# Moving the mask sign, two wide scalings and the centring of weight rows from VectorE to ScalarE, with a new order of the first two tiles

## The chip, the cores and the metric

The kernel runs on one core of one Trainium2 chip. It is one launch. The metric is the device time of one execution in microseconds (us). The engines are named as in the profile: PE is TensorE, ACT is ScalarE, DVE is VectorE, POOL is GpSimd and SP is SyncE, which issues all DMAs of this kernel.

## The reference

Three residual layers over x (128 sequences of 32 rows of 1024), all in float32:

```
x = x + cross_attention(layernorm(x), ctx, ctx, mask)   # 32 query heads, 8 key/value heads, 257 keys
x = x + s4(layernorm(x))                                # causal convolution along the 1024 features + D*u
x = x + router_ffn(layernorm(x), A_w, B_w, Wq_w, keys)  # 64 experts of rank 8, top 16, softmax gates
```

- Attention: scores = q k^T / sqrt(32) + mask, softmax over 257 keys, times the values. The context (128, 257, 256) is key and value at once.
- S4: a kernel of 1024 taps is computed from Lambda, p, q, V, B, Ct and the step: a Cauchy sum over 64 states at 1024 roots of unity, then an inverse FFT. It is then convolved causally with each row.
- FFN: z = x A_w^T (512 columns), gated by expert, times B_w^T, times 2. The router is x Wq_w^T keys^T. The kernel takes the mean of each row of A_w and Wq_w away beforehand, so that the layernorm's mean needs no pass of its own.

## The kernel before

**Tiles.** Four sequences make a tile of 128 rows, and there are 32 tiles. For each tile the attention runs in four parts, b = 0 to 3, one for each sequence. `scores(it, b)` is 24 matmuls into the four banks of `ps_s` (three products of a high and a low part of q and k). Then DVE does eight steps `maximum(it, n)` (line 1395: add the mask, store, and take the row's extreme), ACT does eight `exp(it, n)` (line 832), PE turns the result (`pair_chunk`, line 565), ACT copies it out of PSUM (`pair_copy`, line 784) and PE multiplies by the values (`attend`, line 597). `scores(it, b+1)` waits until all eight maxima of part b have been taken, since they read the same banks.

**Stages.** In the steady part (`for it in range(HEAD, TAIL)`, tiles 2 to 30) the attention of tile it runs beside the convolution of tile it-1 and the FFN of tile it-2. The order inside is written out by hand, engine by engine; there is no scheduler at run time. What stands ahead of that loop on each engine is a list of calls, also written out, for tiles 0 and 1 and for the set-up work: the S4 kernel (`s4_step()` takes the next piece of the DVE generator `s4_kernel`), the router product, and the 16 turned half blocks of A_w and B_w (`weight_chunk(j, h)`, then `weight_high` on ACT and `weight_low` on DVE). Each engine works through its own list in order and waits on semaphores, so an instruction whose input is late holds everything behind it on that engine.

**What the change touches.**

- `masks` (line 1200, DVE): changes the sign of the mask.
- `query_means` and `weight_mean(j)` (lines 793 and 806, ACT): a copy in place whose accumulator gives each row's mean. `query_centre` and `weight_centre(j)` (lines 1218 and 1223, DVE) then scale the row back by 1024 and subtract the mean.
- In `s4_kernel` (DVE) the two scalings `w0 = br*lr` and `w1 = br*li` (line 1271, `times`), 128 by 512 each. Behind them stand the two scaled additions (line 1268), the squares and their sum (line 1250), a reciprocal of 128 by 512 (line 1309) and two products, after which `cauchy_sums` (line 523, PE) can run.
- `STAGE` names the three buffers in which weight rows land: `x`, `xr` and `ots` in the profile. `BANKS` says into which of the four PSUM banks `ps_p` each product goes.
- The query path of tile 0: x lands in `xq`, `q_stats` (DVE), `row_scale` (POOL), `q_norm` (ACT), `store_q` and `move_q` (SP, through DRAM), `q_turn` (DVE), `q_high` (ACT), `q_low` (POOL). In between, POOL takes the product with the 257th key (`last_product`, `last_sum`, `last_mask`), whose result goes through DRAM (`store_last`, `turn_last`) to the first maximum.

Of the kernel before, what the change touches and what calls it, by code (L numbers as in the profile page):

```python
# [18 lines left out]
ALU = mybir.AluOpType  # L19
# [33 lines left out]
S4 = {"cauchy": 31, "sums": 33, "hat": 71, "dft": 72, "column": 77, "rows": 78}  # L53
# [23 lines left out]
    "keys": (1,),  # L77
    "router": (2,),
    "sums": (2,),
    "dft": (1,),  # L80
    "rows": (0,),
    "strip": (1, 3, 0,),
    "w": (1, 0, 1, 3, 2, 1, 0, 2, 3, 2, 2, 3, 0, 2, 2, 2,),
# [27 lines left out]
def build(nc, io):  # L111
    ctx = ExitStack()
    with ctx:
# [136 lines left out]
        su_step = sem("su_step")  # L250
        su_s4 = sem("su_s4")
# [63 lines left out]
        def _(sp):  # L315
# [176 lines left out]
        def _(pe):  # L492
# [252 lines left out]
            keys_transpose(); router_product(); weight_chunk(0, 0); weight_chunk(0, 1); weight_chunk(1, 0)  # L745
            scores(0, 0); weight_chunk(1, 1); scores(0, 1); cauchy_sums(); pair_chunk(0, 0); pair_chunk(0, 1)
# [444 lines left out]
        def _(dve):  # L1191
# [530 lines left out]
```

## Time and profile before

| | us |
|---|---|
| median of 3 runs | 1307.82 |
| lowest and highest | 1303.91, 1310.32 |
| the profiled execution | 1306.38 |
| its span in the profile | 1304.6 |
| PE busy in the span | 1243.8 (95%) |
| ACT busy | 1117.4 (86%) |
| DVE busy | 1057.6 (81%) |
| POOL busy | 827.7 (63%) |

The span is the stretch between the first and the last instruction; the execution's time is 1.8 us longer. The share of busy time is an average over the start, the steady part and the end. In the profile's 40 slices of 32.6 us each, PE stands at 2, 5 and 7 tenths in the first three and at 9 from the fourth on. TensorE's granted clock is at full speed in all slices but the second (9 tenths) and the third (7 tenths).

### The profile page before, as it was taken

The numbers are of one execution on the slowest core, as the hardware profiler recorded it, in microseconds if no ns is written. First come the engines' busy times: TensorE is split into PE (matmuls) and PEld (weight loads), VectorE is DVE, ScalarE is ACT, GpSimd is POOL, SyncE is SP. The second block draws the span as 40 slices with busy tenths as digits, with TensorE's granted clock in tenths as the row PEclk, the third lists the DMA queues.
The fourth block names the chain that finished last, engine by engine and source line by source line (L and its number), as shares of the span: only waits on it lengthen the run. The fifth ranks groups of instructions, "written<-read, shape, count | busy, mean of one in ns | idle before, by whom it ended". The sixth has DMA issues, their size and how long they took to land.

```text
span 1304.6 us, 42153 instructions
## 1 busy us (share of the span) xinstructions
PE 1243.8 (95%) x13676; PEld 1078.2 (83%) x13676; DVE 1057.6 (81%) x3560; ACT 1117.4 (86%) x3329; POOL 827.7 (63%) x1259
## 2 busy tenths in 40 slices
PE   2579999999999999999999999999999999999997
PEld 2457888888888888888888888888888888888876
DVE  6988888888888887888888888887888888888753
ACT  3689989989999998999999898988999898998841
POOL 5437667666666776666677666667766666776420
PEclk9979999999999999999999999999999999999999
DMA  8544454454455455445545454454545445554210
GB/s 211 138 121 121 136 150 121 128 145 130 124 133 140 121 136 137 134 125 131 137 120 146 127 148 117 125 137 128 141 125 145 125 121 141 127 142 120 61 59 33
DMA packets 270940, 166.45 MB, mean 128 GB/s; under 512 B 195433, under 2 KB 253298, under 8 KB 270722
## 3 DMA queue, kind: packets, MB, share of 16 engines
q1 hardware_dynamic: 270722, 163.74, 46.7%
q8 instruction: 112, 1.84, 0.6%
q14 instruction: 106, 0.87, 0.2%
HBM read 128.50 MB, written 34.08 MB: 125 GB/s over the span
## 4 chain that ended last, share of the span: by engine, by line
PE 85%; DVE 4%; SPq 3%; ACT 2%; issue 2%; DMA 2%; POOL 1%; DVEq 0%; POOLq 0%; ACTq 0%
PE ps_p L565 25%; PE ps_p L651 15%; PE ps_p L636 15%; PE ps_p L664 14%; PE ps_p L597 9%; PE ps_s L577 8%; SPq L384 2%; ACT pr L832 1%; DVE ms L1395 1%; DMA dn<-den 1%; DMA turn<-lasts 1%; DVE x L1250 0%; POOL lastp L1095 0%; ACT pts L784 0%; SPq L431 0%
## 5 line engine op out<-in xcount | busy, mean ns | idle before, releaser
L832 ACT ACTIVATE pr<-ms,negmax 128x256 f32<-128x256 f32 x1024 | 513.9, 504 | 12.0 <-DVE negmax L1395 11.9
L1395 DVE CUSTOM_DVE_ANT_0 ms<-ps_s,neg_mask,last 128x256 f32<-128x256 f32 x1024 | 456.6, 470 | 35.4 <-PE ps_s L577 29.9
L784 ACT ACTIVATE pts<-ps_p 128x512 f32<-128x512 f32 x512 | 295.9, 592 | 48.3 <-PE ps_p L565 44.2
L565 PE MATMUL ps_p<-ident,pr 128*128 128x128 f32 x2048 | 306.2, 278 | 9.4 <-DVE wa_lo L1195 4.5
L565 PEld LDWEIGHTS ps_p<-ident,pr 128*128 128x128 f32 x2048 | 240.1, 141 | 44.7 <-issue 16.7
L832 ACT ACTIVATION_READ_ACCUMULATOR pr<-ms,negmax 128x1 f32 x1024 | 199.8, 195 | 0.0
L1053 POOL TENSOR_TENSOR kt<-kr,kt 128x512 fp32r<-128x512 f32 x128 | 165.1, 1290 | 28.4 <-ACT kt L784 27.9
L651 PE MATMUL ps_p<-wa_hi,ut_hi 128*128 128x288 f32 x512 | 177.6, 347 | 1.6 <-DVE ut_lo L1195 1.6
L651 PE MATMUL ps_p<-wa_lo,ut_hi 128*128 128x288 f32 x512 | 151.2, 295 | 0.0
L651 PE MATMUL ps_p<-wa_hi,ut_lo 128*128 128x288 f32 x512 | 150.6, 294 | 0.0
L1095 POOL TENSOR_TENSOR lastp<-lastp 128x256 f32<-128x256 f32 (+4 forms) x320 | 129.7, 405 | 22.7
L597 PE MATMUL ps_p<-pts,cx 128*32 128x128 f32 x4096 | 139.2, 277 | 0.1
L636 PE MATMUL ps_p<-strip_hi,ut_hi 128*128 128x512 f32 (+2 forms) x384 | 138.3, 360 | 0.4 <-DVE tmp L1485 0.4
L577 PE MATMUL ps_s<-kt,qs 32*128 32x256 f32 x3072 | 127.8, 297 | 8.0 <-DVE negmax L1395 5.7
L636 PE MATMUL ps_p<-strip_hi,ut_lo 128*128 128x512 f32 (+2 forms) x384 | 133.4, 347 | 0.0
L636 PE MATMUL ps_p<-strip_lo,ut_hi 128*128 128x512 f32 (+2 forms) x384 | 133.3, 347 | 0.0
L1076 POOL TENSOR_TENSOR qs<-qr,qs 128x512 fp32r<-128x512 f32 x64 | 83.3, 1301 | 69.9 <-ACT qs L784 69.9
L577 PEld LDWEIGHTS ps_s<-kt,qs 32*128 32x128 f32 x3072 | 101.5, 187 | 30.0 <-issue 29.8
L784 ACT ACTIVATE ut_hi<-ps_p 128x512 fp32r<-128x512 f32 x128 | 76.2, 595 | 56.5 <-PE ps_p L565 56.4
L597 PEld LDWEIGHTS ps_p<-pts,cx 128*32 128x32 f32 x4096 | 104.6, 110 | 21.4 <-issue 16.1
L1060 POOL TENSOR_SCALAR lns<-lns 128x1 f32<-128x1 f32 x96 | 18.4, 192 | 158.2 <-DVE lns L1434 157.9
L664 PE MATMUL ps_p<-wb_hi,zt_hi 128*128 128x512 f32 x256 | 111.7, 436 | 3.0 <-DVE zt_lo L1195 3.0
(140 smaller groups left out, 2717.3 us busy)
## 6 DMA issues: line engine op xcount, KB each, us to landing
kx<-in_ctx SPq DMA_DIRECT2D x512, 64.0 KB, 2.4
cx<-in_ctx SPq DMA_DIRECT2D x128, 256.0 KB, 3.1
xq<-in_x SPq DMA_DIRECT2D x32, 512.0 KB, 4.3
turn_q<-xq SPq DMA_DIRECT2D x32, 512.0 KB, 3.8
qx<-turn_q SPq DMA_DIRECT2D x128, 128.0 KB, 2.9
xr<-in_x SPq DMA_DIRECT2D x32, 512.0 KB, 4.3
out_x<-tmp SPq DMA_DIRECT2D x32, 512.0 KB, 5.2
dn<-den SPq DMA_DIRECT2D x512, 2.0 KB, 2.2
```

What stands on the lines that cost most here:

```text
L565: mm = pe.transpose(into[:, j * P:(j + 1) * P], source, ident[:, :])
L577: mm = pe.matmul(ps_s[:, quad, h * SW:(h + 1) * SW], qs[rs, it % 2, q_part, b, h, :, :].rearrange("p r s -> p (r s)"), kt[rs, b, k_part, h ...
L597: mm = pe.matmul(product("o", b, it)[HEAD_DIM * q:HEAD_DIM * (q + 1), h * P:(h + 1) * P], cx[:, b, j, g * HEAD_DIM:(g + 1) * HEAD_DIM], pt ...
L636: mm = pe.matmul(product("y", k, tile)[:, o0:512], u[:, c, :], s[:, s0:s0 + w], start=(c == 0 and j == 0), stop=(c == 4 * k + 3 and j == 2 ...
L651: mm = pe.matmul(product("f", k, tile)[:, 0:ZB], u[:, c, :], w[:, c, k * ZB:(k + 1) * ZB], start=(c == 0 and j == 0), stop=(c == FC - 1 an ...
L664: mm = pe.matmul(product("b", k, tile)[:, :], u[:, c, :], w[:, c, k * 512:(k + 1) * 512], start=(c == 0 and j == 0), stop=(c == BC - 1 and ...
L784: return act.activation(out, in_, ACT.Copy, scale=scale)
L832: act.activation(pr[:, b % 2, g, :], ms[:, n % MS, :], ACT.Exp, bias=negmax[:, n % MS:n % MS + 1], scale=-1.0, accum_out=den[:, b, g:g + 1 ...
L1053: pool.tensor_tensor(kt[:, b, 1, :, 0:2 * P], kr[:, :, :], kt[:, b, 0, :, 0:2 * P].bitcast(F32), ALU.subtract).then_inc(kl_done, 1)
L1076: pool.tensor_tensor(qs[:, tile % 2, 1, :, h, :, :], qr[:, :, :, :], qs[:, tile % 2, 0, :, h, :, :].bitcast(F32), ALU.subtract).then_inc(q ...
L1095: pool.tensor_tensor(near, near, far, ALU.add).then_inc(ls_done, 1)
L1395: dve.tensor_tensor_reduce(ms[:, n % MS, :], ps_s[:, g % GPH, g // GPH * SW:(g // GPH + 1) * SW], neg_mask[:, 0:SW], 1.0, last[:, it % 2, ...
```

## The change

- The mask's sign, the centring of Wq_w and of the four blocks of A_w, and the two wide scalings leave DVE for ACT. The mean is now accumulated with a negative sign, and the centring is `Identity(-1024 * row + bias)`. The scalings are a `Copy` with a scale from `lam`, signalled by a new semaphore `su_wide`, on which DVE waits ahead of the two scaled additions.
- The written lists of all five engines for tiles 0 and 1 are replaced, with the banks of the set-up products and the tile-0 strips. The steady loop and the end are the same as before.

```diff
-S4 = {"cauchy": 31, "sums": 33, "hat": 71, "dft": 72, "column": 77, "rows": 78}
+S4 = {"cauchy": 29, "sums": 31, "hat": 69, "dft": 70, "column": 75, "rows": 76}
...
-    "w": (1, 0, 1, 3, 2, 1, 0, 2, 3, 2, 2, 3, 0, 2, 2, 2,),
+    "w": (0, 2, 0, 1, 2, 3, 2, 2, 3, 2, 1, 2, 3, 0, 1, 3,),
...
-            load_x(0); load_s4(); load_weight(0); load_router(); load_keys(0, 0); load_mask(); clear_kernel()
-            load_wide(); load_last(0); load_weight(1); store_q(0); load_keys(0, 1); load_weight(2); move_q(0)
-            load_keys(0, 2); store_last(0); load_weight(3); load_context(0, 0); load_keys(0, 3); load_x(1)
...
+            load_s4(); load_x(0); load_router(); load_wide(); load_context(0, 2); load_mask(); load_keys(0, 0)
+            load_last(0); load_weight(0); load_keys(0, 1); store_q(0); clear_kernel(); load_weight(1)
+            load_weight(2); move_q(0); load_x(1); load_keys(0, 2); load_weight(3); store_last(0); load_context(0, 0)
+            turn_last(0); load_keys(0, 3); load_context(0, 3); load_last(1); load_keys(1, 0); store_q(1)
+            load_weight(4); load_keys(1, 1); move_q(1); load_x(2); load_context(0, 1); move_den(0, 0)
+            load_weight(5); load_keys(1, 2); load_weight(6); load_weight(7); store_last(1); load_keys(1, 3)
...
             def query_means():
                 act.wait_ge(router_loaded, 32)
-                act.activation(wq_sb, wq_sb, ACT.Copy, scale=1.0 / DIM,
+                act.activation(wq_sb, wq_sb, ACT.Copy, scale=-1.0 / DIM,
                                accum_out=row_mean[0:ROUTER, BC:BC + 1]).then_inc(query_mean, 1)
+
+            def masks():
+                act.wait_ge(m_loaded, 16)
+                copy(neg_mask[:, :], mask_raw, -1.0).then_inc(su_mask, 1)
+
+            def query_centre():
+                act.wait_ge(query_mean, 1)
+                act.activation(wq_sb, wq_sb, ACT.Identity, scale=-float(DIM),
+                               bias=row_mean[0:ROUTER, BC:BC + 1]).then_inc(query_centred, 1)
+
+            def weight_centre(j):
+                act.wait_ge(a_mean, j + 1)
+                act.activation(stages[STAGE[j]], stages[STAGE[j]], ACT.Identity, scale=-float(DIM),
+                               bias=row_mean[:, j:j + 1]).then_inc(a_centred, 1)
+
+            def wide_products():
+                act.wait_ge(wide_loaded, 32)
+                act.wait_ge(su_s4, 2)
+                for j in range(2):
+                    act.activation(work[j], wide[2], ACT.Copy, scale=lam[:, j:j + 1]).then_inc(su_wide, 1)
...
-            def masks():
-                dve.wait_ge(m_loaded, 16)
-                dve.tensor_scalar(neg_mask[:, :], mask_raw, -1.0, None, ALU.mult).then_inc(su_mask, 1)
-                dve.wait_ge(su_mask, 1)
...
-            def query_centre():
-                dve.wait_ge(query_mean, 1)
-                dve.tensor_scalar(wq_sb, wq_sb, float(DIM), row_mean[0:ROUTER, BC:BC + 1], ALU.mult,
-                                  ALU.subtract).then_inc(query_centred, 1)
-
-            def weight_centre(j):
-                dve.wait_ge(a_mean, j + 1)
-                dve.tensor_scalar(stages[STAGE[j]], stages[STAGE[j]], float(DIM), row_mean[:, j:j + 1], ALU.mult,
-                                  ALU.subtract).then_inc(a_centred, 1)
...
-                dve.wait_ge(wide_loaded, 32)
                 ar, ai, br, bi = wide
                 w0, w1 = work
                 lr, li = lam[:, 0:1], lam[:, 1:2]
-                times(w0, br, lr)
-                times(w1, br, li)
-                yield
+                dve.wait_ge(su_wide, 2)
                 scaled(w0, bi, li, w0, ALU.subtract)
                 scaled(w1, bi, lr, w1, ALU.add)
                 yield
```

PE's list up to the second group of scores, before. The names are the outputs and inputs of each instruction; line 513 is the router product, 565 with `x`, `xr`, `ots` a turned weight block, 577 the scores, 523 the Cauchy sums:

```order
L513 MATMUL ps_p<-zg,pts 128x64 x8
L565 MATMUL ps_p<-ident,x 128x128 x8
L565 MATMUL ps_p<-ident,xr 128x128 x4
L577 MATMUL ps_s<-kt,qs 128x256 x24
L565 MATMUL ps_p<-ident,xr 128x128 x4
L577 MATMUL ps_s<-kt,qs 128x256 x24
L523 MATMUL ps_p<-x 128x16 x8
```

The same place now, where line numbers are one higher:

```order
L514 MATMUL ps_p<-zg,pts 128x64 x8
L566 MATMUL ps_p<-ident,x 128x128 x8
L524 MATMUL ps_p<-x 128x16 x8
L566 MATMUL ps_p<-ident,xr 128x128 x8
L578 MATMUL ps_s<-kt,qs 128x256 x24
L566 MATMUL ps_p<-ident,ots 128x128 x4
L566 MATMUL ps_p<-ident,pr 128x128 x4
L566 MATMUL ps_p<-ident,ots 128x128 x4
L566 MATMUL ps_p<-ident,pr 128x128 x4
L578 MATMUL ps_s<-kt,qs 128x256 x24
```

The Cauchy sums and both halves of weight block 1 now stand ahead of the first scores, and block 2 (`ots`) ahead of the second.

ACT's list around the first exponential (line 832 before, 853 now); 806 and 827 are means, 808 a centring, 846 and 867 the normalisation of the queries, 784 and 785 copies. Before:

```order
L806 ACTIVATE ots,top<-ots 128x1024
L784 ACTIVATE kt<-kr 128x512
L784 ACTIVATE qs<-qr 128x4x128
L832 ACTIVATE pr,den<-ms,negmax 128x256
L784 ACTIVATE wa_hi<-ps_p 128x4x128 x2
L784 ACTIVATE kt<-kr 128x512
```

Now:

```order
L808 ACTIVATE xr<-xr,top 128x1024
L785 ACTIVATE qs<-qr 128x4x128
L785 ACTIVATE wa_hi<-ps_p 128x4x128
L827 ACTIVATE ots,top<-ots 128x1024
L785 ACTIVATE qs<-qr 128x4x128
L827 ACTIVATE x,top<-x 128x1024
L808 ACTIVATE ots<-ots,top 128x1024
L785 ACTIVATE wa_hi<-ps_p 128x4x128
L867 ACTIVATE xq<-xq,lns 128x512
L785 ACTIVATE wa_hi<-ps_p 128x4x128
L785 ACTIVATE kt<-kr 128x512
L853 ACTIVATE pr,den<-ms,negmax 128x256 x2
```

The fourth mean (`x`), three of the four centrings, block 1's two copies and half of tile 1's normalisation stand ahead of the first exponential now. At the very start of ACT's list, `wide_products` stands ahead of tile 0's normalisation.

DVE's list up to the first maximum (line 1395 before, 1401 now), from the first turn of the queries, before:

```order
L1408 STREAM_TRANSPOSE qr<-qx 128x512
L1223 TENSOR_SCALAR xr<-xr,top 128x1024
L1250 TENSOR_TENSOR un<-un 128x512
L1309 RECIPROCAL un<-un 128x512
L1431 BN_STATS lns<-xq 128x6 x2
L1395 ISA ms,negmax<-ps_s,neg_mask,last 128x256
```

Now:

```order
L1313 RECIPROCAL un<-un 128x512
L1408 STREAM_TRANSPOSE kr<-kx 128x8x2x32
L1414 STREAM_TRANSPOSE qr<-qx 128x512
L1217 TENSOR_TENSOR wa_lo<-ps_p,wa_hi 128x8x64
L1257 TENSOR_TENSOR x<-x,un 128x512 x2
L1437 BN_STATS lns<-xq 128x6
L1217 TENSOR_TENSOR wa_lo<-ps_p,wa_hi 128x4x128 x2
L1414 STREAM_TRANSPOSE qr<-qx 128x512
L1322 COPY x<-ps_p 128x8x4 x2
```

The whole chain of the S4 kernel up to the Cauchy sums now stands ahead of the second turn of the queries (the second `qr` row), where before it stood behind it.

## Rows read from the trace of the kernel before

**Rows 1.** Windows: span stretch, busy PE, PEld, DVE, ACT, POOL, PEclk, DMA share, GB/s.
```profile
0.00:37.00 37.00, 9.72 (x57) 7.95 (x57) 26.58 (x47) 11.88 (x21) 19.39 (x34) 1.00 0.82 203
37.00:80.00 43.00, 26.87 (x245) 22.97 (x249) 41.37 (x136) 35.35 (x103) 17.63 (x29) 0.83 0.47 126
80.00:116.00 36.00, 31.69 (x365) 24.08 (x354) 28.16 (x93) 32.31 (x97) 23.25 (x36) 0.91 0.53 142
180.00:220.00 40.00, 40.00 (x442) 34.69 (x444) 33.52 (x112) 36.35 (x110) 27.85 (x43) 1.00 0.45 125
```

**Rows 2.** Timeline of PE: start, us, instruction, idle before and its releaser.
```profile
30.79 1.11 PE L565 MATMUL ps_p<-ident,xr 128*128 128x128 f32 x4 [11.02 <-DVE xr L1223]
31.96 1.66 PE L577 MATMUL ps_s<-kt,qs 32*128 32x256 f32 x24
...
42.20 3.60 PE L523 MATMUL ps_p<-x 128*128 128x16 f32 x16 [0.17 <-DVE x L1250]
...
77.79 1.65 PE L577 MATMUL ps_s<-kt,qs 32*128 32x256 f32 x24 [2.21 <-POOL qs L1076]
...
116.23 0.98 PE L577 MATMUL ps_s<-kt,qs 32*128 32x256 f32 x24
```

**Rows 3.** The removed DVE instructions by line: duration ns min/median/max, first and last start.
```profile
L1218 DVE TENSOR_SCALAR pts<-pts,top x1: 741/741/741, 10.7 to 10.7; 16x1024 f32<-16x1024 f32 x1
L1200 DVE TENSOR_SCALAR neg_mask<-ms x1: 298/298/298, 13.2 to 13.2; 128x257 f32<-128x257 f32 x1
L1271 DVE TENSOR_SCALAR un<-tmp,x x2: 1262/1315/1368, 13.9 to 15.2; 128x512 f32<-128x512 f32 x2
L1223 DVE TENSOR_SCALAR x<-x,top x2: 1215/1412/1609, 16.5 to 48.4; 128x1024 f32<-128x1024 f32 x2
L1223 DVE TENSOR_SCALAR xr<-xr,top x1: 1410/1410/1410, 29.3 to 29.3; 128x1024 f32<-128x1024 f32 x1
L1223 DVE TENSOR_SCALAR ots<-ots,top x1: 1798/1798/1798, 42.5 to 42.5; 128x1024 f32<-128x1024 f32 x1
```

**Rows 4.** ACT's means and normalisations by line, same columns.
```profile
L806 ACT ACTIVATE x<-x x2: 1040/1042/1044, 10.5 to 43.9; 128x1024 f32<-128x1024 f32 x2
L846 ACT ACTIVATE xq<-xq,lns x4: 797/800/803, 11.6 to 47.3; 128x512 f32<-128x512 f32 x4
```

**Rows 5.** Timeline of DVE, 13 to 53 us.
```profile
17.68 1.72 DVE L1268 SCALAR_TENSOR_TENSOR un<-tmp,x,un 128x512 f32<-128x512 f32 x2
19.31 0.70 DVE L1402 STREAM_TRANSPOSE kr<-kx 128x512 f32<-128x512 f32 x1
...
24.22 1.40 DVE L1250 TENSOR_TENSOR un<-x 128x512 f32<-128x512 f32 x2
...
30.66 1.75 DVE L1250 TENSOR_TENSOR un<-un 128x512 f32<-128x512 f32 x1
32.44 3.35 DVE L1309 RECIPROCAL un<-un 128x512 f32<-128x512 f32 x1
...
36.85 0.47 DVE L1395 CUSTOM_DVE_ANT_0 ms<-ps_s,neg_mask,last 128x256 f32<-128x256 f32 x1
...
40.78 1.37 DVE L1250 TENSOR_TENSOR x<-x,un 128x512 f32<-128x512 f32 x2
...
50.75 1.46 DVE L1250 TENSOR_TENSOR x<-x 128x8 f32<-128x8 f32 x6
```

**Rows 6.** Issues of DMAs in the first 14 us: KB each, median us to landing.
```profile
tmp<-in_wide SPq DMA_DIRECT2D x1, 512.0 KB, 6.8
```

**Rows 7.** Timeline of ACT at the first exponential.
```profile
37.36 0.51 ACT L832 ACTIVATE pr<-ms,negmax 128x256 f32<-128x256 f32 x1 [7.29 <-DVE negmax L1395]
...
37.87 0.58 ACT L784 ACTIVATE wa_hi<-ps_p 128x512 fp32r<-128x512 f32 x1
```

**Rows 8.** ACT's waits from 36 to 125 us: total, times, longest.
```profile
ACT pr L832 <- DVE negmax L1395: 9.6, 6, 7.3
ACT kt L784 <- DVE kr L1402: 2.2, 2, 2.0
```

More of the change, by code:

```diff
@@ L76 @@
     "o": (3, 2, 1, 1,),
[L77 to L82, printed above, removed]
-    "w": (1, 0, 1, 3, 2, 1, 0, 2, 3, 2, 2, 3, 0, 2, 2, 2,),
+    "keys": (3,),
+    "router": (3,),
+    "sums": (1,),
+    "dft": (0,),
+    "rows": (1,),
+    "strip": (2, 3, 2,),
+    "w": (0, 2, 0, 1, 2, 3, 2, 2, 3, 2, 1, 2, 3, 0, 1, 3,),
 }
@@ L250, in build @@
         su_step = sem("su_step")
+        su_wide = sem("su_wide")
         su_s4 = sem("su_s4")
@@ new lines, in _ @@
+            weight_chunk(1, 0); weight_chunk(1, 1); scores(0, 0); weight_chunk(2, 0); pair_chunk(0, 0)
+            weight_chunk(2, 1); pair_chunk(0, 1); scores(0, 1); weight_chunk(3, 0); pair_chunk(0, 2)
+            pair_chunk(0, 3); weight_chunk(3, 1); pair_chunk(0, 4); weight_chunk(4, 0); scores(0, 2)
+            weight_chunk(4, 1); attend(0, 0); attend(0, 1); pair_chunk(0, 5); pair_chunk(0, 6); weight_chunk(5, 0)
+            weight_chunk(5, 1); pair_chunk(0, 7); dft_product(); pair_chunk(0, 8); scores(0, 3); weight_chunk(6, 0)
@@ L760, in _ @@
+            pair_chunk(1, 4); attend(1, 0); attend(1, 1); pair_chunk(1, 5); pair_chunk(1, 6); pair_chunk(1, 7)
+            pair_chunk(1, 8); attend(1, 2); attend(1, 3); u_chunk(0, 0); scores(1, 3); u_chunk(0, 1)
+            pair_chunk(1, 9); convolve(0, 0, 0, 4); convolve(0, 1, 0, 2); pair_chunk(1, 10); convolve(0, 1, 2, 8)
+            z_chunk(0, 0, 0); z_chunk(0, 1, 0)
             for it in range(HEAD, TAIL):
@@ L1017, in _ @@
-            exp(1, 20); exp(1, 21); q_high(2, 0); exp(1, 22); last_exp(1, 1); exp(1, 23); pair_copy(1, 9)
-            exp(1, 24); k_high(2, 1); exp(1, 25); pair_copy(1, 10); exp(1, 26); q_high(2, 1); exp(1, 27); exp(1, 28)
-            exp(1, 29); z_high(0, 0); exp(1, 30); z_high(0, 1); last_exp(1, 2); exp(1, 31); pair_copy(1, 11)
-            last_exp(1, 3); k_high(2, 2)
+            step_exp(); query_means(); keys_copy(); wide_products(); q_norm(0, 0); q_norm(0, 1); masks()
+            query_centre(); k_high(0, 0); weight_mean(0); weight_centre(0); router_high(); weight_high(0, 0)
@@ new lines, in _ @@
+            weight_mean(1); k_high(0, 1); weight_centre(1); q_high(0, 0); weight_high(0, 1); weight_mean(2)
+            q_high(0, 1); weight_mean(3); weight_centre(2); weight_high(1, 0); q_norm(1, 0); weight_high(1, 1)
+            k_high(0, 2); exp(0, 0); exp(0, 1); weight_high(2, 0); q_norm(1, 1); exp(0, 2); exp(0, 3)
+            weight_centre(3); k_high(0, 3); pair_copy(0, 0); exp(0, 4); exp(0, 5); pair_copy(0, 1)
+            weight_high(2, 1); exp(0, 6); pair_copy(0, 2); exp(0, 7); weight_high(3, 0); exp(0, 8); last_exp(0, 0)
@@ L1021, in _ @@
+            exp(1, 22); k_high(2, 1); exp(1, 23); exp(1, 24); exp(1, 25); exp(1, 26); exp(1, 27); last_exp(1, 2)
+            q_high(2, 1); pair_copy(1, 10); exp(1, 28); exp(1, 29); z_high(0, 0); exp(1, 30); z_high(0, 1)
+            exp(1, 31); k_high(2, 2); pair_copy(1, 11); last_exp(1, 3)
             for it in range(HEAD, TAIL):
@@ L1392, in maximum @@
                     dve.wait_ge(e_done, at(it, STEPS, n + 1 - MS))
+                if it == 0 and n == 0:
+                    dve.wait_ge(su_mask, 1)
                 if it == 0 and n == 2:
@@ new lines, in _ @@
+            q_stats(2, 0); maximum(1, 0); weight_low(6, 1); maximum(1, 1); maximum(1, 2); maximum(1, 3)
+            maximum(1, 4); weight_low(7, 0); k_turn(1, 2); maximum(1, 5); maximum(1, 6); maximum(1, 7)
+            q_stats(2, 1); q_stats(2, 2); k_turn(1, 3); strip_low(0); maximum(1, 8); normalisers(0); maximum(1, 9)
+            maximum(1, 10); k_turn(2, 0); maximum(1, 11); maximum(1, 12); maximum(1, 13); maximum(1, 14)
+            strip_low(1); maximum(1, 15); strip_low(2); out_half(0, 0); maximum(1, 16); out_half(0, 1)
@@ L1653, in _ @@
+            z_low(0, 1)
             for it in range(HEAD, TAIL):
```

122 lines of the change are left out of this document (49 added, 73 removed).

## The prediction

> **What bounds the kernel now.** I read the windows first. In the steady part PE is busy for all of 40.00 us out of 40, while DVE has 33.52 and ACT 36.35: PE is the bound there [rows 1]. The change leaves that loop alone, so all it can do is bring the start of the loop forward or put it back. The loop begins where PE starts the scores of tile 2, at 116.23 us [rows 2]. Until 116 us PE is busy for 9.72 + 26.87 + 31.69 = 68.3 us only, so some 48 us of the start is waiting [rows 1]. That is the stock from which anything can be gained.
>
> The windows also say who fills the start. From 0 to 37 us nobody is full: this is latency, of DMAs and of chains from engine to engine. From 37 to 80 us DVE is busy 41.37 of 43 us, and it is the bound. From 80 to 116 us ACT takes over with 32.31 of 36, PE is at 31.69 and DVE at 28.16 [rows 1]. ACT's own waits after 36 us agree: 9.6 us for DVE's maxima, 7.3 of them ahead of the very first exponential, and 2.2 us for turned keys, again from DVE [rows 7, 8]. So a us taken from DVE before 80 us should move everything behind it, as long as ACT can follow.
>
> **What leaves DVE.** The centring of Wq_w 0.74, the mask 0.30, two scalings of 1.315, and the centrings of A_w 1.22 + 1.41 + 1.80 + 1.61: 9.71 us in eight instructions [rows 3]. Of these 1.80 and 1.61 stand behind the first maximum, at 42.5 and 48.4 us, in the stretch where DVE is the bound: 3.4 us. The other 6.3 us stand before it.
>
> **What ACT gets.** A mean over 1024 columns is 1.04 us without pointer operands, the normalisation of 512 columns with two of them 0.80 [rows 4]. A centring has one, so it lies between 1.04 and about 1.3 (1.04 plus the 0.3 by which 0.80 exceeds half of a mean, 0.52); I take 1.1, five times 5.5 us. The scalings have one pointer and 512 columns: between 0.52 and 0.80, I take 0.6 each, 1.2 us. The mask is at most the 0.51 us of an exponential of about that width [rows 7]. Together about 7 us. Up to 37 us ACT is busy 11.88 us only [rows 1], and all but one centring stand there, so they are covered; the fourth (1.1 us) stands behind the first exponentials. If that cover were gone, the 7 us would be paid whole.
>
> **The new start.** Two chains meet at the first scores.
> 1. S4 chain. The second wide table took 6.8 us from issue to landing [rows 6]. It is issued as the seventh transfer now, at about 3.6 us, and the first A_w block, the keys and the mask no longer stand ahead of it: landing near 10, with 9 and 13.9 (today's first scaling) as bounds. ACT's scalings end near 11.2. DVE then needs 1.72 (two scaled additions), 0.70 (a turn), about 1.5 for two more additions (taken as less than the 1.72), 1.40 (squares), 1.75 (their sum), 3.35 (reciprocal), two turns of 0.70, a low part as wide as a turn, 0.7, and 1.37 (two products) [rows 5]: 13.9 us, so 25 us. The first of those turns of queries may still wait for the queries to come back from DRAM; I add 1.5 for it, between 0 and 3, so 26.5. PE's Cauchy sums take 3.60, two half blocks 1.11 each and the scores 1.66 [rows 2]: 34.0.
> 2. Query chain. It ends today at 31.96 with the scores [rows 2]. POOL's key part moves behind its product with the last key, ACT's normalisation behind the scalings, and DVE's second turn behind the two products; I take the same 31 to 32, so it is not the later one.
>
> The first maximum comes at 34.4 instead of 36.85 [rows 5]: 2.4 us. Today it waits for DVE itself, which is in the reciprocal (32.44 to 35.7) while the scores have long been there [rows 2, 5].
>
> **What is ahead by then.** At 34.4 us DVE has done more than before at 36.85: the two products 1.37, the first complex product 1.46 [rows 5], one low part 0.7 and two small copies of the sums, between 0 and 0.5, taken as 0.4: together 3.9 us. With the 3.4 us that never come, DVE's lead is 2.4 + 3.9 + 3.4 = 9.7 us through the stretch that it bounds.
>
> ACT must follow. Its first exponential comes at about 35.1 instead of 37.36 [rows 7], 2.3 us. Ahead of it stand a mean 1.04, half a normalisation 0.80 and two copies of 0.58 that stood behind it [rows 4, 7], and behind it one centring of 1.1 more: 3.0 - 1.1, another 1.9 us, taken as 1.8 since ACT's instructions overlap a little. That makes 4.1. The other 5.6 us must come from ACT's waits: between 37 and 80 us it is idle for 43 - 35.35 = 7.65 us [rows 1], and most of that is for work of DVE, which comes earlier now. So 9.7 is possible without ACT being full, and from 80 us ACT has 3.7 us more of idle time [rows 1] as a reserve. PE has 16 us idle from 37 to 80, and its 3.60 us of Cauchy sums have left that stretch. I take 9.5 us, since new waits for PSUM banks (half blocks and pairs share four, and each block's bank is freed by a low part on DVE) eat a little. The upper end is 9.7 plus the reserve, 13; the lower end, if ACT recovers half of the 5.6, is 6.9.
>
> **A rule against it.** The two scalings took 1.26 and 1.37 us, while the mask, half as wide, took 0.30 [rows 3]: by width alone they would be about 0.6 each. They ran beside POOL. The Trainium skill (SBUF — State Buffer, "SBUF: two separate sides") says that VectorE and GpSimd share one pair of ports, and that the first to come holds it for its whole instruction, against single-input VectorE instructions in a fast mode as against those with two SBUF inputs, while ScalarE has ports of its own. By that rule ScalarE's 0.6 is safe, but the scaled additions behind, with two inputs in SBUF, inherit the wait.
>
> **The sum.** The profiled execution took 1306.38 us; less 9.5 that is 1296.9. The median of the runs is 1.4 us above it, so by the median 1298.3, which I predict; the rivals' times are by the median too.
>
> **The rivals.**
> - *Inherited port waits.* Of the 9.7 us that leave DVE, 2.63 - 1.2 = 1.4 for the scalings, and 1.80 + 1.61 + 1.41 - 3 x 1.22 = 1.2 for the centrings, were not the instructions' own work [rows 3]. If the next instruction waits in their place, 2.6 us come back: a gain of 6.9, 1300.9. For it: 1.72 for two scaled additions against 1.40 for two squares [rows 5]. Against it: POOL is busy 17.63 of 43 us in the stretch that counts [rows 1]. Chance 0.15.
> - *PE or SP as the new head of the line.* PE turns weight blocks ahead of scores now, and blocks 5 to 7 are issued by SP behind `load_x(2)`, which waits for POOL's product of tile 1. If block 5 is late, PE stands in front of it with pairs, the DFT and the fourth scores behind. The price is one landing, 5 to 6 us, bounded by the 6.8 of such a transfer [rows 6]: a gain of 3.5 to 4.5, 1304. For it: today 11.02 us of PE's waiting are for one weight block [rows 2]. Chance 0.18.
> - *The lead is given back at the loop's door.* If ACT (32.31 of 36 [rows 1]) cannot shorten its stretch, because its waits there are for PE's strips, the maxima run ahead and stop after eight. Gain 0 to 3: 1306.3 in the middle. Chance 0.10.
> - *Slower.* ACT's head. `wide_products` stands ahead of tile 0's normalisation, and the fourth mean and tile 1's normalisation ahead of the first exponential. If the wide table lands as late as today (13.9 [rows 3]) the normalisation moves by 3.5 us, then the turns of the queries; if the fourth block lands 5 us after the scores, exp(0,0) starts at about 44. From there ACT's own 67.7 us of work up to 116 us [rows 1], less 1.8, end at 110 plus the waits; with today's 11.3 us of waits kept, the loop starts at 121, 5 us late: 1313. It decides from exp(0,0) at 39.2 on if no wait goes, and from 50 on if all go. Against it: 37 us in which ACT is one third busy. Chance 0.07.
>
> **How the numbers follow.** The forecast has 0.50: 1298.3, on its own from 1294.8 (13 us) to 1300.9 (6.9 us). The rest is with the four rivals. A measurement tells about 0.5% from nothing, that is 6.5 us, so faster means under 1301.3. The forecast gives 0.46 to faster and 0.04 to the same; the port waits give 0.09 and 0.06, the late block 0.03 and 0.15, the returned lead 0 and 0.10, and the slower rival 0.02 to the same and 0.05 to slower. Faster 0.58, same 0.37, slower 0.05. The range reaches down to 1294.5, the 13 us end, and up to 1305.5, where the slower rival and most of the returned lead are left out.
>
> **What would show it.** Right: the scores of tile 2 start near 107 us; the first maximum near 34.4 and the first exponential near 35; Cauchy sums on PE near 26.5; DVE below nine tenths nowhere between 37 and 70; the scores of tile 1, today at 77.79 [rows 2], near 68. Wrong: a first maximum later than 37, a wait of PE for a weight block's DMA over 3 us, scaled additions over 2.5 us the pair, or a lead at tile 1's scores that is gone at tile 2's. If the lead is there at tile 2 and the time does not show it, the steady part has changed, which I exclude, since its lists are the same.

## The result

The kernel after the change took 1293.14 us in the median of 4 runs (1291.56 to 1294.01); the kernel before, run beside it, 1306.57 us (4 runs). The ratio is 0.9894, with a 95% interval of 0.9866 to 0.9922: faster by about 1.1%. The prediction was 1298.3 us with a range from 1294.5 to 1305.5. The direction is right; the gain is larger than forecast, and the time lies 1.4 us below the range. The same kernel timed a second time gave 1291.18 us against 1302.46, ratio 0.9912 [0.9896, 0.9929]. By the two comparisons the gain is 13.4 and 11.3 us. The forecast was 9.5. Single executions of one kernel lie up to 9 us apart, so 1 to 2 us between two of them say little by themselves.

### The profile after

The profiled execution took 1292.63 us, its span is 1290.8 us. The windows (stretch of the span, length, then busy time of PE, PEld, DVE, ACT and POOL with counts, PEclk, DMA share, GB/s) answer to [rows 1]:

```profile
0.00:37.00 37.00, 15.85 (x85) 13.72 (x85) 28.42 (x67) 23.61 (x43) 20.33 (x39) 1.00 0.80 220
37.00:80.00 43.00, 30.14 (x366) 23.15 (x367) 37.56 (x138) 39.95 (x124) 19.30 (x32) 0.92 0.60 148
80.00:116.00 36.00, 30.63 (x372) 25.95 (x374) 29.98 (x101) 33.74 (x101) 26.83 (x41) 1.00 0.48 129
180.00:220.00 40.00, 40.00 (x472) 34.68 (x465) 33.96 (x113) 36.11 (x111) 27.12 (x41) 1.00 0.51 127
```

In the first 37 us PE and ACT do 6.1 and 11.7 us more work than in [rows 1]. From 37 to 80 us DVE has come down from 41.37 to 37.56 us, and ACT has risen from 35.35 to 39.95 of 43. The steady part is as full of PE as before. PE's timeline (start, us, instruction, in brackets the idle time before it and its releaser) answers to [rows 2]:

```profile
25.23 3.60 PE L524 MATMUL ps_p<-x 128*128 128x16 f32 x16 [5.73 <-DVE x L1257]
28.66 1.95 PE L566 MATMUL ps_p<-ident,xr 128*128 128x128 f32 x8
30.54 1.65 PE L578 MATMUL ps_s<-kt,qs 32*128 32x256 f32 x24
...
66.27 0.99 PE L578 MATMUL ps_s<-kt,qs 32*128 32x256 f32 x24
...
104.61 0.98 PE L578 MATMUL ps_s<-kt,qs 32*128 32x256 f32 x24
```

The Cauchy sums moved from 42.20 to 25.23 us, ahead of the first scores. The scores of tile 1 start 11.5 us earlier than in [rows 2], those of tile 2, where the loop begins, 11.6 us earlier. DVE's timeline, which answers to [rows 5]:

```profile
11.06 1.54 DVE L1275 SCALAR_TENSOR_TENSOR un<-tmp,x,un 128x512 f32<-128x512 f32 x2 [1.63 <-ACT un L815]
12.63 0.71 DVE L1408 STREAM_TRANSPOSE kr<-kx 128x512 f32<-128x512 f32 x1
13.27 2.38 DVE L1275 SCALAR_TENSOR_TENSOR x<-x,un 128x512 f32<-128x512 f32 x2
15.69 1.97 DVE L1257 TENSOR_TENSOR un<-x 128x512 f32<-128x512 f32 x2
17.69 0.70 DVE L1257 TENSOR_TENSOR un<-un 128x512 f32<-128x512 f32 x1
18.42 3.35 DVE L1313 RECIPROCAL un<-un 128x512 f32<-128x512 f32 x1
...
23.78 1.40 DVE L1257 TENSOR_TENSOR x<-x,un 128x512 f32<-128x512 f32 x2
...
32.32 0.48 DVE L1401 CUSTOM_DVE_ANT_0 ms<-ps_s,neg_mask,last 128x256 f32<-128x256 f32 x1
```

This is a chain with nearly no gap: from the first scaled addition at 11.06 to PE's Cauchy sums at 25.23 are 14.17 us. The first maximum stands at 32.32 us, 4.5 us earlier. On ACT, first the moved scalings and the mask (timeline), and then the centrings of A_w by line (duration ns min/median/max, first and last start), where [rows 3] had them on DVE:

```profile
9.69 1.33 ACT L815 ACTIVATE un<-tmp,x 128x512 f32<-128x512 f32 x2 [2.20 <-DMA tmp<-in_wide]
10.93 1.51 ACT L867 ACTIVATE xq<-xq,lns 128x512 f32<-128x512 f32 x2
12.35 0.40 ACT L785 ACTIVATE neg_mask<-ms 128x257 f32<-128x257 f32 x1
12.65 1.13 ACT L803 ACTIVATE pts<-pts,top 16x1024 f32<-16x1024 f32 x1
...
33.88 0.50 ACT L853 ACTIVATE pr<-ms,negmax 128x256 f32<-128x256 f32 x1
```

```profile
L808 ACT ACTIVATE x<-x,top x2: 1141/1144/1148, 16.3 to 37.0; 128x1024 f32<-128x1024 f32 x2
L808 ACT ACTIVATE xr<-xr,top x1: 1132/1132/1132, 23.3 to 23.3; 128x1024 f32<-128x1024 f32 x1
L808 ACT ACTIVATE ots<-ots,top x1: 1136/1136/1136, 29.2 to 29.2; 128x1024 f32<-128x1024 f32 x1
```

ACT's waits from 34 to 115 us (engine, tile, releaser: total, times, longest), for [rows 8]. The 9.6 us of waiting for DVE's maxima have become 1.6, and the first exponential, which waited 7.29 us in [rows 7], has no marked wait. The longest that are left:

```profile
ACT pr L853 <- DVE negmax L1401: 1.6, 2, 1.3
ACT pts L785 <- PE ps_p L566: 1.3, 3, 0.5
ACT ut_hi L785 <- PE ps_p L566: 1.0, 1, 1.0
```

### One stretch, cut at the right places

Fixed windows cut each kernel at another point of its work. Cut from the first maximum to the first scores of tile 2, the stretch holds the same maxima in every kernel. Before:

```profile
36.85:116.23 79.38, 58.79 (x604) 47.12 (x604) 69.86 (x227) 67.89 (x201) 41.09 (x64) 0.87 0.50 133
```

After:

```profile
32.32:104.61 72.29, 52.26 (x589) 40.77 (x588) 61.04 (x213) 67.53 (x203) 40.37 (x61) 0.95 0.59 150
```

The stretch is 7.1 us shorter. DVE's work in it is 8.8 us less (69.86 to 61.04, 14 instructions fewer); its idle time is 1.7 us more (79.38 - 69.86 = 9.5, and 72.29 - 61.04 = 11.2). ACT's work is unchanged. So the 11.6 us at tile 2 are 4.5 us of an earlier first maximum and 7.1 us of a shorter stretch behind it. This cut is used for all experiments below:

| kernel | time, us (runs) | ratio to before | first maximum | scores of tile 2 | DVE busy between | DVE idle between |
|---|---|---|---|---|---|---|
| before | (above) | 1 | 36.85 | 116.23 | 69.86 | 9.5 |
| after | 1293.14 (4) | 0.9894 [0.9866, 0.9922] | 32.32 | 104.61 | 61.04 | 11.2 |
| e5 after, again | 1291.18 (4) | 0.9912 [0.9896, 0.9929] | 33.88 | 106.36 | 61.52 | 11.0 |
| e1 moves only | 1301.89 (10) | 0.9985 [0.9969, 1.0001] | 35.91 | 113.83 | 66.57 | 11.4 |
| e2 order only | 1299.26 (10) | 0.9955 [0.9938, 0.9971] | 34.47 | 109.06 | 64.15 | 10.4 |
| e3 scalings back | 1294.11 (4) | 0.9916 [0.9883, 0.9949] | 34.33 | 105.36 | 61.79 | 9.2 |
| e4 centrings back | 1300.35 (10) | 0.9962 [0.9945, 0.9978] | 35.07 | 110.03 | 64.16 | 10.8 |
| e6 before, DVE +3.3 | 1307.02 (5) | 1.0032 [1.0016, 1.0047] | 36.04 | 119.65 | 72.85 | 10.8 |
| e7 after, DVE +3.3 | 1295.20 (2) | 0.9946 [0.9926, 0.9966] | 33.07 | 107.94 | 65.19 | 9.7 |
| e8 after, ACT +3.2 | 1293.28 (2) | 0.9931 [0.9911, 0.9951] | 33.89 | 106.09 | 60.62 | 11.6 |
| e9 products on POOL | 1295.13 (6) | 0.9928 [0.9908, 0.9949] | 33.84 | 104.62 | 59.30 | 11.5 |
| e10 e9, scalings back | 1291.35 (4) | 0.9904 [0.9889, 0.9919] | 33.34 | 104.30 | 59.27 | 11.7 |
| e11 before, strips later | 1307.25 (7) | 1.0024 [1.0009, 1.0040] | 36.03 | 116.44 | 69.88 | 10.5 |
| e12 before, ACT +3.3 | 1306.62 (10) | 1.0017 [1.0004, 1.0031] | 35.86 | 116.51 | 69.02 | 11.6 |

The ratios are to runs of the kernel before beside each group: its median was 1304.03 us (25 runs) for e1 to e4, 1302.46 (10) for e5 to e8, and 1303.77 (20) for e9 to e12. The last four columns are from one profiled execution each, and that of the kernel before (1306.38 us) was slower than these medians. DVE's idle time stays between 9.2 and 11.7 us while its work goes from 59 to 73 us: to some 2.5 us, the length of this stretch follows DVE's work.

One pair of executions is not enough for the first maximum. Up to it, e6, e11 and e12 have the lists of before, and e5, e7 and e8 those of after. It stands at 36.85, 36.04, 36.03 and 35.86 us in the four executions with the old lists, and at 32.32, 33.88, 33.07 and 33.89 in the four with the new ones. By the medians that is 2.6 us earlier; the 4.5 us above set the latest old one against the earliest new one.

### The profile page after: what moved, and what is told of

It is laid out like the page before. It is cut to its first block, busy times and chain, and to the rows that moved or that the text cites. A ratio compares the mean times of both kernels' runs of the same rounds, so it can differ in the third digit from the quotient of the medians.

```text
span 1290.8 us, 42154 instructions
## 1 busy us (share of the span) xinstructions
PE 1238.7 (96%) x13676; PEld 1074.4 (83%) x13676; DVE 1046.6 (81%) x3552; ACT 1122.5 (87%) x3337; POOL 824.7 (64%) x1259
## 4 chain that ended last, share of the span: by engine, by line
PE 86%; DVE 4%; SPq 3%; issue 2%; DMA 2%; ACT 2%; POOL 1%; DVEq 0%; ACTq 0%; POOLq 0%
PE ps_p L566 25%; PE ps_p L637 16%; PE ps_p L652 15%; PE ps_p L665 14%; PE ps_p L598 9%; PE ps_s L578 8%; SPq L385 2%; DVE ms L1401 1%; DMA dn<-den 1%; ACT pr L853 1%; DVE x L1257 0%; DMA qx<-turn_q 0%; SPq L373 0%; DMA vl<-in_ctx 0%; PE ps_p L524 0%
```

## The experiments

### e1: the moves alone

```diff
-            s4_step(); q_stats(0, 0); q_stats(0, 1); s4_step(); q_stats(0, 2); s4_step(); query_centre()
-            k_turn(0, 0); s4_step(); masks(); s4_step(); weight_centre(0); s4_step(); k_turn(0, 1); s4_step()
+            s4_step(); q_stats(0, 0); q_stats(0, 1); s4_step(); q_stats(0, 2); s4_step()
+            k_turn(0, 0); s4_step(); s4_step(); s4_step(); k_turn(0, 1); s4_step()
```

(The first lines of VectorE's list of before; the other centrings go likewise, and ScalarE's list of before takes up the same steps.)

> The lists of before, with the mask sign, the two wide scalings and the centring on ScalarE. Theory (VectorE's work bounds the start up to about 80 us, so what leaves it behind the reciprocal counts in full): 1.4 us of centring ahead of the first maximum and 3.4 us behind it go, so the scores of tile 2 start at about 111.4 us instead of 116.2, a gain of about 5 us. Rival (the order is what counts): the scores of tile 2 start within 1 us of 116.2.

Measured: the loop starts 2.4 us earlier, where about 5 were expected, and the time is 2.1 us below before, with 1 inside the interval of the ratio. DVE's work in the stretch fell by 3.3 us, as priced, but its idle time rose by 1.8; new are 2.1 us of maxima that wait for ACT's exponentials. The first maximum, at 35.91, is where e6, e11 and e12 have it without any move.

### e2: the order alone

```diff
-                dve.wait_ge(su_wide, 2)
+                dve.wait_ge(wide_loaded, 32)
+                times(w0, br, lr)
+                times(w1, br, li)
```

(with the mask and the centrings on DVE too, in the new lists)

> The new lists and banks, with all of the moved work on VectorE, each centring at a place where the new list has room. Theory: 9.7 us return to VectorE, of which some 3 to 4 fall into its waits for the wide table and for the Cauchy sums; the scores of tile 2 start at about 110 us, a gain of 5 to 7 us against before. Rival (the order is what counts): they start within 1.5 us of the 104.6 of the changed kernel, a gain of over 11 us.

Measured: the loop starts 7.2 us earlier (5 to 7 were expected), the time is 4.8 us below before. The first maximum stands at 34.47, 2.4 us earlier than in before's profile, and DVE's work behind it is 5.7 us less (227 instructions before, 215 here), with the same instructions in the program. About 2.9 of the 5.7 us now stand ahead of the first maximum, in the time that is latency: the two products (1.3), six small products (1.2) and the two copies (0.4). Another 2.7 are the centrings: one stands ahead of the first maximum now, and the one behind it took 0.75 us, where the two behind it took 1.80 and 1.61 before ([rows 3]). The order is the larger part, and part of its gain is that instructions take less time in their new places.

### e3 and e4: each move taken back

```diff
-            step_exp(); query_means(); keys_copy(); wide_products(); q_norm(0, 0); q_norm(0, 1); masks()
+            step_exp(); query_means(); keys_copy(); q_norm(0, 0); q_norm(0, 1); masks()
```

That is e3, ScalarE's list; VectorE scales again ahead of its additions. In e4 the five centrings go back:

```diff
-            q_stats(1, 2); s4_step(); weight_low(1, 0); maximum(0, 0); maximum(0, 1); maximum(0, 2); maximum(0, 3)
+            q_stats(1, 2); weight_centre(2); s4_step(); weight_low(1, 0); maximum(0, 0); maximum(0, 1); maximum(0, 2); maximum(0, 3)
```

> The changed kernel with the two wide scalings back on VectorE. Theory: VectorE waits for the table at that place anyway and GpSimd is idle until 13.6 us, so the two take about 0.6 us each instead of the 1.3 of before, and the scores of tile 2 start at 104.6 plus or minus 0.7 us. Rival (they cost VectorE their 2.6 us wherever they stand): the reciprocal ends 1.3 us later, at 23, and so does all behind it.

> The changed kernel with the five centrings back on VectorE. Theory: of their 6.6 us about 2.5 fall into VectorE's waits (Wq_w before the wide table, block 1 during the Cauchy sums); the scores of tile 2 start about 3.5 us later than 104.6, at 108. Rival (ScalarE is the bound since it took them): ScalarE loses 5.5 us of work and the loop starts no later than 104.6.

Measured, e3: at tile 2 it lies between the two executions of the changed kernel, and its ratio (0.9916) cannot be told from theirs. The move of the scalings is worth nothing that can be told. Its DVE timeline says why:

```profile
11.47 1.01 DVE L1272 TENSOR_SCALAR un<-tmp,x 128x512 f32<-128x512 f32 x2 [2.02 <-DMA tmp<-in_wide]
12.51 1.54 DVE L1269 SCALAR_TENSOR_TENSOR un<-tmp,x,un 128x512 f32<-128x512 f32 x2
```

Both scalings took 1.01 us together there, against 2.63 in [rows 3]. POOL was idle from 9.9 to 15.7 us in this kernel; in the kernel before, POOL's key product (13.67 to 14.93) and its last product (14.89 to 16.33) ran beside them.

Measured, e4: the loop starts 3.7 to 5.4 us later than in the changed kernel's two executions (3.5 were expected), and the time is 7 to 9 us above it by the medians, 6 above e3 that was timed beside it. The first maximum comes 1.2 to 2.8 us later, and DVE's work behind it is 2.6 to 3.1 us more. Of the moves, that of the centrings is the one that counts. But only one centring stands behind the first maximum in e4, and it took 0.75 us:

```profile
40.56 0.75 DVE L1230 TENSOR_SCALAR x<-x,top 128x1024 f32<-128x1024 f32 x1
41.23 2.86 DVE L1257 TENSOR_TENSOR x<-x 128x8 f32<-128x8 f32 x6
45.28 2.54 DVE L1257 TENSOR_TENSOR x<-x 128x8 f32<-128x8 f32 x6
```

The same two groups of small products in e5, the changed kernel again:

```profile
39.45 2.19 DVE L1257 TENSOR_TENSOR x<-x 128x8 f32<-128x8 f32 x6
42.79 1.27 DVE L1257 TENSOR_TENSOR x<-x 128x8 f32<-128x8 f32 x6
```

They are 1.9 us shorter there. In e4 the second group (45.28 to 47.8) runs into POOL's product of 45.50 to 46.78, and one of the six, from 45.68 to 46.80, takes 1.12 us instead of 0.17; in e5 the group is over before POOL's product starts at 44.46. So most of what the centrings cost behind the first maximum is where they push the small products; that the overlap with POOL is the reason is argued from these times, not tested.

### e5: the changed kernel again

> The changed kernel once more, beside runs of the kernel before on the same chip. Theory (the gain of 13.4 us is about 11.6 us at the start of tile 2 and about 2 us that come and go between executions with the clock and the landing of the first transfers): a gain of 11 to 12 us. Rival (something after the start is shorter too): 13 to 14 us again.

Measured: 1291.18 us, a gain of 11.3 us as the theory said, and in the profile (its slowest run, 1294.35 us) a first maximum at 33.88, 1.6 us later than in the first. The whole difference is there when DVE begins its reciprocal (18.42 and 19.95). The wide table was there 0.7 us later (ACT's scalings at 10.37 rather than 9.69), and DVE then waited 0.89 us for a key block:

```profile
11.74 1.54 DVE L1275 SCALAR_TENSOR_TENSOR un<-tmp,x,un 128x512 f32<-128x512 f32 x2 [1.67 <-ACT un L815]
14.17 0.71 DVE L1408 STREAM_TRANSPOSE kr<-kx 128x512 f32<-128x512 f32 x1 [0.89 <-DMA kx<-in_ctx]
14.80 2.38 DVE L1275 SCALAR_TENSOR_TENSOR x<-x,un 128x512 f32<-128x512 f32 x2
```

So landings move the start by 1.6 us between executions of one kernel. Behind the first maximum the two agree (72.29 and 72.48 us to tile 2).

### e6, e7 and e8: which engine bounds

```diff
+            def extra_dve():
+                dve.reciprocal(work[0], work[0])
+            def extra_act():
+                act.wait_ge(su_s4, S4["cauchy"])
+                for n in range(3):
+                    act.activation(un[:, :], un[:, :], ACT.Copy).then_inc(probe, 1)
+                    act.wait_ge(probe, n + 1)
```

The reciprocal stands in the kernel before at 49 us (e6) and in the changed kernel behind maximum(0, 10) (e7), the copies in the changed kernel at 46.5 us (e8). Their results are used by nothing.

> The kernel before with one more reciprocal of 128 by 512 (3.35 us) on VectorE at about 48 us, on a buffer that nothing reads. Theory (VectorE is the bound there): the scores of tile 2 start 3 us or more later, at 119.3. Rival (latency between engines bounds the start): under 1.5 us later.

> The changed kernel with the same reciprocal (3.35 us) on VectorE at about 41 us. Theory (VectorE and ScalarE are now about equally full): the scores of tile 2 start 2 to 3 us later than 104.6. Rival (ScalarE alone bounds it now): under 1 us later.

> The changed kernel with three more copies of 128 by 1024 (3.3 us together) on ScalarE at about 44 us. Theory: ScalarE is busy 9.8 of 10 us there, so the scores of tile 2 start 2.5 to 3.3 us later than 104.6. Rival (ScalarE has slack, VectorE is still the bound): under 1 us later.

Measured: 3.34 us more on DVE made before's stretch 4.2 us longer (79.38 to 83.61; against the stretches of e11 and e12, 80.41 and 80.65, it is 3.0 to 3.2), and the changed kernel's 2.4 to 2.6 us longer (74.87). That is what the theories of e6 and e7 said. 3.2 us more on ACT left the changed kernel's stretch as it was (72.20), against the expectation: ACT's work in it rose by 2.0 to 2.4 us and used up idle time, though ACT is the busier of the two engines there.

### e9 and e10: a version with less on DVE

```diff
-                prod12 = cmul(0, s[1], s[2])
-                yield
-                num = cmul(2, prod12, one_w)
-                yield
-                mr, mi = cmul(4, s[3], one_w)
-                yield
+                num = (c8[:, 2, :], c8[:, 3, :])
+                mr, mi = c8[:, 4, :], c8[:, 5, :]
+                link[0] = S4["mr"]
```

(VectorE's side; GpSimd makes the three products in three steps of its own.)

> The changed kernel, with the three small complex products behind the Cauchy sums (18 dependent operations on 8 columns) taken from VectorE and issued on GpSimd. Theory (VectorE's queue sets the speed between the first maximum and the first scores of tile 2, and some 4.6 us of it go away): the first scores of tile 2 stand 2 to 4 us earlier than the 104.6 and 106.4 of the changed kernel's two executions, and the time is 2 to 4 us below its 1291 to 1293, at 1287 to 1290. Rival (the place of the small products is hidden by now, or GpSimd gets to them too late, so that VectorE waits for them before the hat): no gain, within 1 us, or up to 3 us later.

> As the kernel with the small products on GpSimd, but the two wide scalings stand on VectorE again, as before the change. Theory: the scalings cost VectorE about 1 us before the Cauchy sums when nothing runs beside them, and ScalarE is spared as much, so both kernels agree within 1.5 us. Rival (the scalings' move is what pulled the first maximum to 32 to 34): 2 to 3 us slower than the kernel with the products alone.

Measured: e9's reciprocal starts at 19.93 us and its first maximum at 33.84, e5's at 19.95 and 33.88, so these two executions can be set side by side: DVE's work behind the first maximum is 2.2 us less in e9, and tile 2 starts 1.7 us earlier (104.62 against 106.36). What is taken from DVE there still counts, but it is less than the 2 to 4 expected, since the first of the three products (1.11 us at 30.50 after) already stood ahead of the first maximum. Taking it away there brought nothing: the first maximum then waited 0.80 us for PE's scores. Against the changed kernel's first execution, with its better landings, there is no gain at tile 2. At tile 2 e10 agrees with e9 within 0.3 us, as expected. By time e10 is 1291.35 and cannot be told from the changed kernel; e9 is 1295.13, with runs from 1289.81 to 1298.87, and its profiled execution took 1291.97. Why e9's runs scatter so is open. No version here is shown to beat the changed kernel.

### e11: one rearrangement by itself

```diff
-            strip_part(0); strip_part(1); strip_part(2); weight_chunk(6, 1); attend(0, 4); attend(0, 5)
+            weight_chunk(6, 1); attend(0, 4); attend(0, 5)
-            pair_chunk(0, 12); pair_chunk(0, 13); pair_chunk(0, 14); scores(1, 1); pair_chunk(0, 15)
+            pair_chunk(0, 12); pair_chunk(0, 13); pair_chunk(0, 14); scores(1, 1)
+            strip_part(0); strip_part(1); strip_part(2); pair_chunk(0, 15)
```

(TensorE's list; the strips' copies on ScalarE and VectorE move behind with them.)

> The kernel before, with one thing of the new order: the three strip parts of TensorE, and the copies of them on ScalarE and VectorE, stand behind the scores (1,1) rather than ahead of them. Theory (the new order gains mostly at these two places): the scores (1,1), before at 89.7, start near 86, and the first scores of tile 2, before at 116.2, 1 to 3 us earlier; the time is 1 to 3 us below the kernel before. Rival (VectorE's queue does the same work in either order, and TensorE only waits elsewhere): tile 2 starts within 0.5 us of before and the time is the same.

Measured: the scores (1,1) started at 86.67 instead of 89.69 us, 3.0 earlier, and the scores (1,2) at 95.77 instead of 95.09; tile 2 started at 116.44. The rival was right at tile 2: what TensorE does earlier is given back as long as DVE has the same work behind the first maximum (69.88 against 69.86). The time is not the same: it is 3.5 us above before by the medians, ratio 1.0024 [1.0009, 1.0040]. The profile shows no place for that in the start, so it stays open.

### e12: ScalarE's slack before the change

```diff
-            weight_high(2, 0); pair_copy(0, 2); pair_copy(0, 3); exp(0, 10); exp(0, 11); exp(0, 12); exp(0, 13)
+            weight_high(2, 0); pair_copy(0, 2); pair_copy(0, 3); exp(0, 10); extra_act(); exp(0, 11); exp(0, 12); exp(0, 13)
```

with the three copies of e8.

> The kernel before, with 3.3 us of needless copies on ScalarE at about 50 us. Theory (VectorE bounds this stretch in the kernel before and ScalarE has slack there, as it has in the changed kernel): the first scores of tile 2 stay within 1 us of 116.2 and the time within 1 us of the kernel before. Rival (ScalarE is as tight as VectorE before the change): 2.5 to 3.5 us later and slower.

Measured: tile 2 starts 0.3 us later, as the theory said. The time is 2.8 us above before by the medians, ratio 1.0017 [1.0004, 1.0031], over the 1 us expected; the profiled execution, at 1302.91 us, was one of the fastest of the ten. e8 shows the same: nothing at tile 2, and 2.1 us more by the medians, with intervals that overlap. Whether the copies cost something that these two profiled executions do not show stays open.

## Why the prediction was right and wrong

**The bound and the mechanism: right.** The gain is in the start, DVE sets its pace from the first maximum on (e6, e7, e9, e11), the loop's own period is untouched, and ACT follows. Three of the four rivals fell: no weight block made PE wait for more than 3 us behind the first scores, the lead of tile 1 (11.5 us) was there at tile 2 (11.6), and the first exponential came at 33.88 rather than 44. One sign held only in the mean: DVE was to be below nine tenths nowhere from 37 to 70 us; it was at 29.92 of 33, 0.91, but at 0.88 from 47 to 57.

**The step that failed: the new start.** Two terms of its sum were too large: the 1.5 us of waiting for the queries, which never came, and the 7.9 us from the Cauchy sums on PE to the first maximum, which were 7.1. In the first execution:
- The table was there by 9.69 and DVE's first scaled addition started at 11.06: as forecast, to 0.2 us.
- From there to the Cauchy sums 14.17 us, for 13.9 forecast. Single terms were off and cancelled: the second pair of scaled additions 2.38 for 1.5, the squares 1.97 for 1.40, and their sum 0.70 for 1.75.
- The 1.5 us of waiting did not come. The queries were back; the only gap is 0.20 us at a key. This was the largest error of the start: Cauchy sums at 25.23 instead of 26.5.
- From the Cauchy sums to the first maximum 7.09 us (25.23 to 32.32) for 7.9. PE works through the sums and the eight half-block instructions with overlap (28.66 - 25.23 = 3.43 for 3.60; 1.88 for the two half blocks, forecast at 2.22), and the first maximum starts 1.78 us after the scores do, forecast 2.06.

Together the first maximum comes 2.1 us before the 34.4 of the forecast: 4.5 gained instead of 2.4. The other three executions with the new lists (e5, e7, e8) say which part of that is solid. The wait for the queries is missing in all of them, and from the Cauchy sums to the first maximum they take 7.07 to 7.10 us, not 7.9. But a table or a key landed later there, and the Cauchy sums start at 26.78, 26.00 and 26.81, about where the forecast had them. So their agreement with 26.5 is luck: a wait that never came against landings that came late. The first maximum is then 0.5 to 1.3 us before its forecast, and the rest of the 4.5 us is that the profile of before had its first maximum 0.8 to 1.0 us later than three others with the same lists, and the profile of after 0.8 to 1.6 us earlier than its three.

In the new order DVE is no longer late for the scores: it ends a low part at 32.21 us, PE's scores end at 32.19, and the maximum starts at 32.32. Taking DVE's work away ahead of it brings nothing more, as e9 shows.

**What is ahead by then: right in sum, wrong in its parts.** The forecast was 3.9 us done before the first maximum and 3.4 us of centrings that never come, of which 7.1 us were taken. Measured 7.1 and 6.9 us. But DVE's work fell by 5.7 us with the order alone (e2) and by 3.1 more with the moves (61.04 against e2's 64.15), and 1.7 us of new idle time on DVE stand against them. The steps that come ahead were 2.9 us, not 3.9. The 3.4 us of the two late centrings were mostly not their own work: in the new order they took 0.70 and 0.75 us on DVE (e2). What the moves brought beyond that is in the small products, as e4 shows; the prediction had no term for it. At the start of the loop the two edits add up: 2.4 us (e1) and 7.2 (e2) make 9.6, and together they brought 9.9 and 11.6. By the medians they don't quite, 2.1 and 4.8 against 11.3 and 13.4; how much of that is the scatter of loop and tail that is shown below stays open.

**Port waits: there, but not inherited.** The two scalings on DVE took 1.3 us each beside POOL and 0.5 without it (e3), and the centrings 1.22 to 1.80 us before and 0.70 to 0.94 in the new order (e2). Behind the moved scalings, the second pair of scaled additions and the squares took 2.38 and 1.97 us beside POOL's last product and its sums, 1.45 us over the forecast together, where the rival asked for 2.6. The rival's reason was that the next instructions take over the wait of those that left. That is not so here: in e3, with the scalings back on DVE, the same two took 2.38 and 1.97 us again. In both kernels they stand beside POOL's product (13.60 to 15.10 after, 15.70 to 17.29 in e3) and its sums, where the new order puts them. The Trainium skill (SBUF — State Buffer, "SBUF: two separate sides") says that VectorE and GpSimd share a pair of ports, which one instruction holds to its end while the other waits. The trace agrees in kind: the scalings took 2.63 us beside POOL's products and 1.01 with POOL idle. The chain as a whole still came out near its forecast, since their sum took 0.70 us instead of 1.75.

**ACT: priced right, and not the limit.** A centring took 1.13 to 1.15 us for 1.1 forecast, a scaling 0.71 for 0.6, the mask 0.40. ACT is busy 67.5 of the 72.3 us of the stretch and still does not bound it (e8). The "reserve" from which the range's upper gain was taken was therefore not the limit.

**The rest, 2.1 us, is not the change's.** The profiled executions differ by 13.75 us: 11.6 at tile 2, 12.2 at the last scores of tile 31, and 1.6 in the tail behind them. In the tail of before, TensorE's granted clock was down for part of these 10 us (PEclk is the granted share of full speed, 2.4 GHz; the lower level is 1.2 GHz, and 0.83 is a mixture; it fell after a microsecond in which PE did nothing):

```profile
1262.00:1272.00 10.00, 7.83 (x38) 6.45 (x37) 4.80 (x11) 1.84 (x2) 3.52 (x5) 0.83 0.01 2
```

The same stretch after the change:

```profile
1250.00:1260.00 10.00, 7.83 (x46) 6.55 (x45) 5.17 (x11) 1.96 (x3) 3.52 (x5) 1.00 0.01 2
```

PE did nothing for a microsecond at this point there too (1254 to 1255), and the clock stayed; what decides is not shown. In e5, the same kernel, it was 0.83 again (1248 to 1258), and once more near the end, and its tail took 64.6 us where the first execution took 61.3 and before 62.8. All fourteen profiled executions fall in three groups: no low stretch, a tail of 61.2 to 61.3 us (four); one, 62.7 to 63.0 (eight); two, 64.5 to 64.6 (two), without regard to the kernel. So the tail gives or takes 1.6 or 3.3 us by chance.

The loop gives and takes as well. From the first scores of tile 2 to the last scores the fourteen took 1121.7 to 1126.5 us (before 1125.5, after 1124.9, e5 1121.7), by steps that are longer here and there. In e5 the lead of 9.9 us at tile 2 had grown to 13.7 at the last scores. So the size of the gain in time, 13.4 or 11.3 us, holds some luck of loop and tail; what the change itself brings is read at tile 2, 9.9 to 11.6 us.

**The range.** It ended at 13 us of gain, from ACT's reserve alone (9.7 and 3.7 are in fact 13.4; and 13 us below 1307.8 are 1294.8, where the range has 1294.5). The start had unknowns of its own, written down as 0 to 3 us for the queries and 9 to 13.9 for the landing, and their good ends (1.5 and 1.0 us) were never added to it. With them it would have reached 15.5 us of gain, 1292.3, and held the time. Nor did it have a term for the scatter of loop and tail, which is larger than the miss of 1.4 us.

## What to carry to other kernels

When an engine bounds only a part of the start, count its work between two fixed events (here the first maximum and the first scores of the loop) rather than in fixed windows: its idle time there changed by 2.5 us at most while its work changed by 14, so a us of work that an order moves ahead of the first event, or a move takes away, is worth most of a us at the second. Look also at how long the same instructions take in their new places: here small products cost 1.9 us more or less by where a neighbour's product fell. An instruction that looks slow beside another engine is not worth moving before it has been seen alone. And whatever is bounded from both sides in the working must also be in the range: here the best ends of the waits were left out of it.

## What the runs showed of the hardware that was not expected

- The same two DVE scalings of 128x512 took 2.63 us beside POOL's products and 1.01 us with POOL idle (e3): a factor of 2.6. The reciprocal of the same shape took 3.35 us, beside POOL's sums too (at 18.42 after).
- Six products and sums of 128x8 took 1.11 us on DVE at best (at 30.50 after), up to 2.86 beside POOL's products (e4), and 1.60 or 1.61 us on POOL each time (e9), so for operations as small as that POOL is nearly as quick.
- The loop repeats to 0.01 us: 37.72 to 37.73 us from tile to tile in most of 29 steps. The last of the 29 takes 38.6. Single steps are longer by up to 2.3 us (39.66 once before, 39.07 once after, 40.01 once in e3); e5 has none of these. What causes the slips is open.
- In the tail, a stretch of 3 to 4 us in which TensorE's granted clock is at 0.50 (1.2 GHz) goes with some 1.6 us more of time. The changed kernel had none in one execution and two in another.
